# The aggregate of layer L3 as three products of rounded parts, in a four-layer graph network on one core

## The reference

```
h = relu(layernorm(x)); x = x + L0(h, adj)   # hypergraph convolution, twice
h = relu(layernorm(x)); x = x + L1(h, adj)   # transition matrix T, hops T@h and T@(T@h)
h = relu(layernorm(x)); x = x + L2(h, adj)   # 8 heads: tanh(adj * (Xc Xp^T)) @ Xp, relu
h = relu(layernorm(x)); x = x + L3(h, adj)

def L3(x, a, kernel):
    t = a @ x                     # the aggregate: 512x512 by 512x256
    out = relu(t @ kernel)        # 512x256 by 256x256
    return out * mask             # mask: rows of x that are not all zero
```

## Time and profile before

| | |
|---|---|
| median of 3 runs | 1583.87 us (1582.29 to 1586.97) |
| the profiled execution | 1586.44 us, its span 1584.4 us |
| TensorE matmuls busy | 1458.1 us, 92% of the span |
| VectorE busy | 1192.4 us, 75% |
| ScalarE busy | 884.6 us, 56% |
| GpSimd busy | 285.6 us, 18% |
| HBM | 83.04 MB read, 8.39 MB written, 58 GB/s over the span |
| mean granted TensorE clock | 0.983 of 2.4 GHz |

### The profile page before, as it was taken

How to read it: one execution, slowest core, us unless ns; L and a number is a source line. 1 busy time by engine, 2 the same in 40 slices (tenths; PEclk the granted TensorE clock), 3 DMA queues, 4 the chain that set the end, 5 groups by cost and what they waited for, 6 DMA issues and landing times.

```text
span 1584.4 us, 28215 instructions
## 1 busy us (share of the span) xinstructions
PE 1458.1 (92%) x10426; PEld 1111.6 (70%) x10426; DVE 1192.4 (75%) x2669; ACT 884.6 (56%) x1501; POOL 285.6 (18%) x348
## 2 busy tenths in 40 slices
...
PEclk9789899999999999999999999999999999999998
...
DMA packets 58553, 92.21 MB, mean 58 GB/s; under 512 B 4288, under 2 KB 23296, under 8 KB 58496
## 3 DMA queue, kind: packets, MB, share of 16 engines
q1 hardware_dynamic: 58496, 91.44, 17.5%
...
HBM read 83.04 MB, written 8.39 MB: 58 GB/s over the span
## 4 chain that ended last, share of the span: by engine, by line
PE 65%; issue 16%; DVE 11%; ACT 6%; POOL 2%; DMA 1%; ACTq 0%; POOLq 0%; SPq 0%; DVEq 0%
PE ring_f L1362 40%; PE ring_b L1362 8%; PE ring_b L1645 6%; PE pv_acc L1661 6%; PE ring_f L1539 2%; POOL rstd L501 2%; ACT hf L580 2%; DVE att L1193 1%; ACT uz L570 1%; DVE m L994 1%; DVE bns L953 1%; DVE uz L994 1%; DVE tr_l L994 1%; PE ring_f L1439 1%; DVE rows L1121 1%
## 5 line engine op out<-in xcount | busy, mean ns | idle before, releaser
L1193 DVE TENSOR_TENSOR att<-ring_b,at 128x1024 f32<-128x1024 f32 x256 | 308.1, 1219 | 93.9 <-PE ring_b L1645 89.4
L728 ACT ACTIVATE att<-att 128x1024 f32<-128x1024 f32 x256 | 268.2, 1055 | 164.1 <-DVE att L1193 162.8
L501 POOL TENSOR_TENSOR rstd<-var,mhalf 128x4 f32<-128x4 f32 x80 | 81.7, 1022 | 713.9 <-DVE var L968 713.8
L1362 PE MATMUL ring_f<-w,uz 128*128 128x256 f32 (+1 forms) x896 | 191.0, 335 | 2.4 <-DVE uz L994 1.8
L1362 PE MATMUL ring_f<-m,tr_h 128*128 128x256 f32 x1024 | 190.8, 287 | 0.0
L1362 PEld LDWEIGHTS ring_f<-m,tr_h 128*128 128x128 f32 x1024 | 158.6, 191 | 22.8 <-issue 22.0
L1362 PEld LDWEIGHTS ring_f<-w,uz 128*128 128x128 f32 x896 | 152.1, 192 | 26.2 <-DVE uz L994 7.5
L1362 PEld LDWEIGHTS ring_f<-m,inc_n 128*128 128x128 f32 x1024 | 128.2, 195 | 39.5 <-issue 26.6
L1362 PE MATMUL ring_f<-m,inc_n 128*128 128x256 f32 x1024 | 135.4, 289 | 18.4 <-POOL m L505 16.2
L1362 PE MATMUL ring_f<-m,tr_l 128*128 128x256 f32 x512 | 144.5, 282 | 0.0
L1661 PE MATMUL pv_acc<-att,xp_n 128*32 128x512 f32 x1024 | 134.9, 604 | 4.5 <-ACT att L728 3.5
...
## 6 DMA issues: line engine op xcount, KB each, us to landing
at<-in_adjT SPq DMA_DIRECT2D x32, 1024.0 KB, 6.8
rows<-in_adjT SPq DMA_DIRECT2D x16, 1024.0 KB, 6.2
adj_n<-in_adj SPq DMA_DIRECT2D x16, 1024.0 KB, 5.4
...
```

The costliest lines, as they stand in the source:

```text
L501: pool.tensor_tensor(rstd[k][:], var[k][:], mhalf[:], ALU.pow).then_inc(rstd_made[k].sem, 1)
L728: act.activation(v, v, ACT.Tanh).then_inc(tanh_made.sem, 1)
L1193: dve.tensor_tensor(att[:, u % 2, 2 * half:2 * half + 2], ring_b[half][:], at[:, u % NT].unsqueeze(1).broadcast_to([P, 2, N]), ALU.mult).t ...
L1362: ins = pe.matmul(dst, lhsT, rhs, start=(first and n == 0), stop=(last and n == len(pairs) - 1), skip_group_check=True)
```

## The change

The aggregate of L3 is made as `three` products of parts. The adjacency's parts go into buffers of L1: the high part into `tr_h` (called `at_h`), the low part into `m2` (called `at_l`). The state's parts go into the memory of `tr_l` (`h3_s`), and the parts of the aggregate then overwrite them, so that `ax_s` has another layout (per node tile instead of in one row). ScalarE gets `k_at` twice and `k_h3s` once per graph, VectorE the same. `f_tt` and `f_r` now wait until the aggregate has read the buffers (`ax_full`), `k_at` waits until the hops have (`x2_full`) and until L0 of the next graph but one is through with `m2` (`y_full`). `at2` may be loaded anew once it is split (`at_lo`). All lists of all five engines stand in another order.

```diff
-        ax_s = xc_s.rearrange("p a (c n) -> p (a c) n", c=2)
+        at_h = tr_h
+        at_l = m2[:].rearrange("p a (t n) -> p (a t) n", n=N)
+        h3_s = xc_s.rearrange("p a (t d) -> p a t d", d=D)
+        ax_s = lambda a, c: h3_s[:, a, :, c * P:(c + 1) * P]
...
             def next_at2(g):
...
-                        sp.wait_ge(ax_full.sem, ax_full.after(g, 2, ago=1))
+                        sp.wait_ge(at_lo.sem, at_lo.after(g, 2, ago=1))
...
# ScalarE, f_tt (j == 0) and f_r (k == 0)
+                    if seen(g, 2):
+                        act.wait_ge(ax_full.sem, ax_full.after(g, 2, ago=2))
...
+            def k_at(g, half):
+                v = slice(2 * half, 2 * half + 2)
+                if half == 0:
+                    act.wait_ge(at2_loaded.sem, at2_loaded.after(g, 1))
+                    if seen(g, 1):
+                        act.wait_ge(ax_full.sem, ax_full.after(g, 2, ago=1))
+                    if followed(g):
+                        if seen(g, -1):
+                            act.wait_ge(x2_full.sem, x2_full.after(g, 2, ago=-1))
+                copy(at_h[:, v], at2[:, v], at_hi)
+
+            def k_h3s(g):
+                act.wait_ge(h_made[H3].sem, h_made[H3].after(g, NT))
...
+                copy(h3_s[:, 0], h3[:], h3_hi)
...
# VectorE
+            def k_at(g, half):
...
+                dve.wait_ge(at_hi.sem, at_hi.after(g, half + 1))
+                low(at_l[:, v], at2[:, v], at_h[:, v], at_lo)
+
+            def k_h3s(g):
+                dve.wait_ge(h3_hi.sem, h3_hi.after(g, 1))
+                low(h3_s[:, 1], h3[:], h3_s[:, 0], h3_lo)
...
# TensorE
             def k_ax(g, c, half):
                 if c == 0 and half == 0:
-                    pe.wait_ge(at2_loaded.sem, at2_loaded.after(g, 1))
+                    pe.wait_ge(h3_lo.sem, h3_lo.after(g, 1))
...
                 if c == 0:
-                    pe.wait_ge(h_made[H3].sem, h_made[H3].after(g, 2 * half + 2))
-                ins = products(ax_bank(g, c), [(h3[:, t, c * P:(c + 1) * P], at2[:, t])
-                                               for t in (2 * half, 2 * half + 1)], half == 0, half == 1)
+                    pe.wait_ge(at_lo.sem, at_lo.after(g, half + 1))
+                pairs = []
+                for t in (2 * half, 2 * half + 1):
+                    v = slice(c * P, (c + 1) * P)
+                    pairs += three(h3_s[:, 0, t, v], h3_s[:, 1, t, v], at_h[:, t], at_l[:, t])
+                ins = products(ax_bank(g, c), pairs, half == 0, half == 1)
...
# the loop's list on SyncE
-                    (0, next_x), (2, next_at), (4, store), (3, next_at2), (0, next_adj), (0, next_wrow),
+                    (0, next_x), (0, next_wrow), (3, next_at2), (2, next_at), (4, store), (0, next_adj),
```

More of the change, by code:

```diff
@@ L857, in _ @@
+                (-1, k_h3, 3), (-1, k_h3s), (-1, k_ax, 0), (-1, k_ax, 1), (-1, k_out, 0), (-1, k_out, 1),
             )
@@ new lines, in _ @@
+                (2, f_xw, 0), (0, k_outT, 0), (0, k_outT, 1), (2, f_xw, 1), (0, bn, 4, 0), (0, bn, 4, 1),
+                (0, bn, 4, 2), (0, bn, 4, 3), (0, variance, 4), (2, f_m2, 0), (2, f_m2, 1), (0, offset, 4),
+                (1, k_hT), (2, f_y, 0), (2, f_y, 1), (2, bn, 2, 0), (2, bn, 2, 1), (2, bn, 2, 2), (2, bn, 2, 3),
+                (2, variance, 2), (3, bn, 0, 0), (2, offset, 2), (3, bn, 0, 1), (0, k_at, 0), (0, k_at, 1),
+                (2, f_hT, 0), (2, f_hT, 1), (1, k_split, 0), (1, k_xc), (3, bn, 0, 2), (2, f_q, 0), (0, k_h3s),
@@ new lines, in _ @@
+                (-3, bn, 4, 3), (-3, variance, 4), (-1, f_m2, 0), (-1, f_m2, 1), (-2, k_hT), (-1, f_y, 0),
+                (-1, f_y, 1), (-3, offset, 4), (-1, bn, 2, 0), (-1, bn, 2, 1), (-1, bn, 2, 2), (-1, bn, 2, 3),
+                (-1, variance, 2), (-1, offset, 2), (-3, k_at, 0), (-3, k_at, 1), (-1, f_hT, 0), (-1, f_hT, 1),
+                (-2, k_split, 0), (-2, k_xc), (-1, f_q, 0), (-3, k_h3s), (-1, f_max, 0), (-1, f_q, 1),
+                (-1, f_q, 2), (-1, f_mask, 0), (-3, k_mask), (-1, f_max, 1), (-1, f_mask, 1), (-1, f_q, 3),
@@ L1711, in turn @@
-                    (0, f_m2, 1), (1, k_hT), (2, k_outT, 0), (0, f_y, 0), (2, k_attend, 7), (0, f_y, 1),
-                    (2, k_outT, 1), (1, k_xp, 0), (1, k_xp, 1), (1, k_xc, 0), (1, k_xc, 1), (1, k_xn, 0),
-                    (0, f_hT, 0), (0, f_hT, 1), (1, k_xn, 1), (0, f_sj), (0, f_q, 0), (0, f_q, 1), (2, k_ax, 0, 0),
-                    (0, f_q, 2), (0, f_q, 3), (2, k_ax, 0, 1), (2, k_ax, 1, 0), (2, k_ax, 1, 1), (2, k_out, 0),
+                    (0, f_m, 0), (0, f_m, 1), (2, k_attend, 1), (2, k_scores, 3), (0, f_u, 0), (0, f_u, 1),
```

634 lines of the change are left out of this document (323 added, 311 removed).

## The result

The changed kernel takes 1598.19 us (1597.79 to 1598.63, 4 runs) against 1583.61 us (1582.29 to 1586.97, 4 runs) for the kernel before on the same chip: a ratio of 1.0091, interval 1.0076 to 1.0106. The forecast was 1577, the range ended at 1594. The profiled execution has a span of 1596.3 us, 11.9 more than before's 1584.4.

The account below looks back on a forecast made before the run. TensorE was taken to bound the loop, busy 89.5 of 92.86 us per turn. Ten turns -11, three early turns -7, start +1.8 and tail +9 gave -7 us from 1583.87, so 1577 us; range 1560 to 1594.

Parts of the forecast that it names:

- The products: Aggregate of L3 on TensorE: 24 shorter products take 5.7 us instead of 6.85, 1.15 us less per graph.
- The splitting: Extra 3.7 us on VectorE and 3.2 on ScalarE per graph; neither becomes the bound by its sum, only by place.
- The turn, -1.1: Each turn of the loop gets 1.1 us shorter, between 0 and -2.3; ten turns give -11 us.
- Place A: TensorE's 1.20 us wait ahead of k_xp goes, gain 1.2 us; new waits of 0.7 and 0.9 us, against 0.63 before.
- place B: Stretch from f_hT to f_tt, taking gain back: TensorE waits 0.65 us at the third f_q, 0.35 at the aggregate.
- my sum for it now is 23.6: Stretch from the end of f_y to f_tt: 25.1 us before, 23.6 now; of the 1.5 about 1.1 stays.
- The tail, +9: From graph 15's f_tt to the end: 9 us longer, between +4 and +14, summed as 6.9 + 3.5 - 1.3.
- The start, +1.8: VectorE's offset waits behind inc_n, so TensorE starts at 18.0 us instead of 16.2.
- The early turns, -7: Three turns from graph 2 to 5, 1.2 us longer than later ones, save that too: -2.3 x 3.
- The slower one: VectorE's chain up to f_trans grows by 2.5 us and sets f_tt; turn gains nothing, tail +12, 1595 us; chance 0.15.
- Rival 3: The turn gains 0.7 us, the tail costs 11: no change, 1584 us; chance 0.18.
- Rival 4: Weight loads of the new products lie in the open: +3.4 us a graph, 1637 us; chance 0.01.

Follow-up runs that it names:

- run 1: The changed kernel's new lists, but with the old float32 aggregate of L3 (no k_at, no k_h3s): 1616.1 us, ratio 1.0204 to the kernel before.
- run 2: The three products and the splitting, with the old lists on TensorE, ScalarE, VectorE and GpSimd: 1666.17 us, ratio 1.0517 to the kernel before.
- Runs 5 and 6: Each against the changed kernel: 5 issues k_xp 0's six products twice per loop turn, 1600.39 us; 6 moves k_xn 1 behind f_q 1, 1601.82 us.
- Run 3: The changed kernel with the old lists of TensorE, ScalarE and VectorE behind the last f_tt: 1594.81 us, ratio 1.0071 to the kernel before.
- run 4: The changed kernel with two entries of VectorE's first list moved, the first norm's offset ahead of inc_n again: 1595.95 us, ratio 1.0078 to the kernel before.

## Why the prediction was wrong

**The products: right.** "I take 5.7, so 1.15 us less": 1.02 measured (run 1 against after). In after the group is 240 + 120 instructions at 405 and 397 ns, and a stream of 18 (1000.21 to 1004.48) takes 4.27 us, so (4.27 - 0.40)/17 = 0.23 each, every one with its own load. The Trainium skill's rule ("TensorE: Matmul & The Clock Gate", Part 3, The mechanism) would, by the estimate in the prediction, have put 7.7 us there; the trace does not agree with it here either. (The text above that rule names a background weight buffer as a second way for a load to run ahead, which the rule leaves out; the trace here can't tell how the loads are hidden, only that they are.)

```profile
L1414 PE MATMUL ring_b<-tr_h,tr_l 128*128 128x512 f32 x240 | 82.3, 405 | 10.4 <-DVE tr_l L1028 9.2
...
L1414 PE MATMUL ring_b<-m,tr_l 128*128 128x512 f32 x120 | 47.6, 397 | 0.0
```

**The splitting: right.** "Neither becomes the bound by its sum, only by its place": run 1 shows the same waits without it, run 2 what a bad place costs.

**The turn, -1.1: the step that failed first, by 0.7 us in each of ten turns.** Place A's "gain 1.2 us" was the wait of 1.20 us, and that is gone, but `f_sj` stands only 0.1 us earlier. Ahead of it the text itself names 0.7 and 0.9 in place of 0.63, and place B 0.65 and 0.35. From these terms, -1.2 + 0.7 + 0.27 + 0.65 + 0.35 - 1.15, comes -0.4, not the -1.1 that I took from "my sum for it now is 23.6", a lining-up of the engines whose parts the text does not give. Measured are -0.42. That the two agree is luck in part. With what the terms measured (0.32 for 0.7, 0.44 for 0.27, 0.46 for 0.65, 0 for 0.35, -1.02 for -1.15) they come to -1.0. The 0.6 that lack had no term: 0.22 in the first 68 us, which the forecast put at "net nothing" and where `f_tt` now waits for 0.18; about 0.15 between `k_xp` and `f_sj`, where TensorE is busy for 7.15 us with the work that took 6.94; and about 0.2 behind `f_sj`. So two steps failed here: the sum was not made from the named terms, and the work around a new wait was taken to be as dense as before. With -0.4 in the ten turns and -0.4 - 1.2 in each of the three before, the same working ends at +2 us, 1586, and with the tail as measured at 1594. Runs 5 and 6 show the reason for the small number: between `f_y` and the third `f_q` TensorE waits for the norm, ScalarE and VectorE, so neither 1.2 us less waiting nor 0.5 us less work moves the end.

**The clock in the loop: not foreseen.** The forecast had the clock only as a cost in the tail. One long turn in this profile is 1.3 us of the ten turns' miss.

**The tail, +9 for +16.7.** By its own terms: `k_xp` +5.7, measured 8.2 (1522.54 - 1471.01 against 43.35); the scores behind it +10.1, measured +12.8 (20.17 for 7.42), of which 2.4 are `k_xp` at the half clock behind a wait of 2.94 us that the forecast had as "waits behind VectorE's norm" without asking what TensorE's clock does then; the units -8.9, measured -6.0 (25.1 us for 31.1), since waits of 0.1 to 1.4 us stand between units that were to "run undisturbed"; the last aggregate +3.5 and -1.3, measured +3.4 and -1.6. The mechanism was right in every other step, the sizes were short in three, all to the same side, 8 us together. Run 3, where `k_xp` comes at 44.3 us, gives 7.2 of its 8.2 us to the order of the lists; why that is 2.5 more than forecast was not taken apart.

**The start, +1.8**: right. TensorE began at 18.41 for 18.0, and run 4 gives 1.7 us for the offset; that graph 2 was 1.0 us late in the profile is mixed with the chance of the clock. **The early turns, -7**: -3.6, and about -2.1 with the clock as in before. The forecast took the 1.2 us by which each of these turns was longer, 3.6 in all, as a loss that the loop's lists would save; 1.5 of it was the fall of the clock in one of them.

**The rivals.** The slower one named VectorE's chain up to `f_trans` as the cause; that chain ended in time (the wait ahead of `f_tt` is none). Its time, 1595, came nearest to the 1598 measured, and it had the turn at 0 and the tail at +12; its reason was not the one. Rival 3, "no change", had the turn at -0.7 and the tail at 11. Rival 4's own sum gives 1638, not 1637, and its +3.4 us a graph is four times the 0.8 of the prediction's own part on the products; neither was seen.
